# A new order of the attention stage: contexts in groups, scores later behind the rows of maxima, three more additions per head group, the low half of the maxima from a reduction

## The reference

```python
q = (x @ Wq).reshape(b, n, 4, 4, 32)       # 4 groups of 4 heads, head size 32
k = (x @ Wk).reshape(b, n, 4, 32)
v = (x @ Wv).reshape(b, n, 4, 32)
scores = einsum('bqgsd,bkgd->bgsqk', q, k) / sqrt(32)     # causal: keys behind the query are -inf
attn = softmax(scores, axis=-1)
ctx = einsum('bgsqk,bkgd->bqgsd', attn, v)
```

## Time and profile before

| | |
|---|---|
| median of 3 runs | 2770.99 us (2770.24 to 2773.05) |
| the profiled execution | 2771.73 us, its span 2770.0 us |
| PE busy | 2589.9 us, 93% |
| DVE, ACT, POOL busy | 1713.5, 1436.7, 982.6 us |
| mean granted TensorE clock | 0.96 of full speed |

### The profile page before, as it was taken

The page is one execution under the profiler, slowest core; times in us unless marked ns, Lnnn a source line. Parts: engine busy times, 40 slices in busy tenths (PEclk is TensorE's granted clock), DMA queues, the critical chain, the costliest instruction groups (busy, mean ns, idle before and its releaser), DMA issues. The chain is left out here.

```text
span 2770.0 us, 40600 instructions
## 1 busy us (share of the span) xinstructions
PE 2589.9 (93%) x14178; PEld 1808.6 (65%) x14178; DVE 1713.5 (62%) x3567; ACT 1436.7 (52%) x2768; POOL 982.6 (35%) x601
## 2 busy tenths in 40 slices
PE   6997999999999999999696999999999999699998
PEld 5784545454555545553475788888788888588886
DVE  3225777777777777783496544446554454467776
ACT  1221546555555556565487555556554554345453
POOL 6000455655565656566693000000000000245554
PEclk9996999999999999999897999999999999899999
DMA  6444012121111111110597323225432332675453
GB/s 216 163 163 115 22 34 60 44 60 41 49 47 43 49 49 47 43 33 9 172 347 253 112 85 115 100 91 177 135 111 80 114 103 88 217 254 162 124 164 103
DMA packets 204212, 304.34 MB, mean 110 GB/s; under 512 B 39376, under 2 KB 85488, under 8 KB 199792
## 3 DMA queue, kind: packets, MB, share of 16 engines
q1 hardware_dynamic: 200768, 294.72, 34.0%
q0 software_dynamic: 1600, 5.24, 0.5%
q10 hardware_dynamic: 1648, 1.88, 0.2%
HBM read 184.83 MB, written 116.42 MB: 109 GB/s over the span
## 5 line engine op out<-in xcount | busy, mean ns | idle before, releaser
L782 ACT ACTIVATE p_probs<-p_ps_s 128x512 f32<-128x512 f32 (+3 forms) x1280 | 598.3, 537 | 420.6 <-PE p_ps_s L715 413.4
L809 DVE TENSOR_REDUCE p_parts<-p_ps_m 128x1 f32<-128x512 f32 x768 | 477.4, 681 | 126.7 <-PE p_ps_m L703 126.0
L703 PE MATMUL p_ps_m<-p_k_m,p_q 96*128 96x512 f32 (+3 forms) x1280 | 480.2, 405 | 25.2 <-DMA p_q<-q_t 11.7
L715 PE MATMUL p_ps_s<-p_q,p_k_e 98*128 98x512 f32 (+3 forms) x1280 | 461.5, 386 | 29.1 <-DMA p_q<-p_rows 21.8
L672 POOL TENSOR_TENSOR p_added<-p_added,p_probs 128x2048 f32<-128x2048 f32 x88 | 403.2, 4582 | 32.5 <-ACT p_probs L782 23.9
L703 PEld LDWEIGHTS p_ps_m<-p_k_m,p_q 96*128 96x128 f32 x1280 | 247.8, 198 | 234.9 <-DVE p_parts L809 93.8
L715 PEld LDWEIGHTS p_ps_s<-p_q,p_k_e 98*128 98x128 f32 x1280 | 243.3, 195 | 161.9 <-ACT p_probs L782 70.3
L1671 POOL MEMSET p_power<- 128x1 f32 x1 | 0.1, 98 | 891.0 <-POOLq L1849 891.0
L733 PE MATMUL p_ps_c<-p_probs,p_v 128*32 128x512 f32 (+3 forms) x2560 | 306.8, 552 | 1.1 <-ACT p_probs L782 0.7
L813 DVE CUSTOM_DVE_ANT_0 p_masked<-p_ps_m,p_mask 128x384 f32<-128x384 f32 (+3 forms) x512 | 226.2, 487 | 122.5 <-PE p_ps_m L703 120.2
L73 PE MATMUL p_ps_l<-p_xT_hi,p_mu_hi 128*128 128x512 f32 x512 | 207.7, 406 | 16.4 <-DVE p_xT_lo L1500 11.7
(11 more groups left out here) (181 smaller groups left out, 4678.7 us busy)
## 6 DMA issues: line engine op xcount, KB each, us to landing
logits_t<-p_logit SPq DMA_DIRECT2D x32, 1024.0 KB, 5.0
p_lg<-logits_t SPq DMA_DIRECT2D x128, 256.0 KB, 3.7
p_q<-q_t SPq DMA_DIRECT2D x96, 256.0 KB, 4.7
p_w_raw<-L_ffn_W_dram SPq DMA_DIRECT2D x64, 256.0 KB, 5.4
p_so<-slot_out SPq DMA_DIRECT2D x32, 512.0 KB, 6.6
p_x<-L_attn_x_dram SPq DMA_DIRECT2D x8, 1024.0 KB, 6.3
q_t<-p_f_hi SPq DMA_DIRECT2D x32, 256.0 KB, 2.5
q_t<-p_f_lo SPq DMA_DIRECT2D x32, 256.0 KB, 2.6
```

The costliest lines, as they stand in the source:

```text
L703: pe.matmul(ps_m[:, u % M_BANKS, 0:w], q[0:QROWS, qb, h, bass.ts(t, P)], k_m[:, c * BLK:c * BLK + w], start=True, stop=True).then_inc(s_un ...
L715: pe.matmul(ps_s[:, u % ST_BANKS, q0:BLK], k_e[:, bass.ts(kt, P)], q[:, qb, h, q0:BLK], start=True, stop=True).then_inc(s_score, 1)
L782: act.activation(probs[s % RING][:, h, q0:BLK], ps_s[:, u % ST_BANKS, q0:BLK], ACT.Exp).then_inc(s_exp, 1)
L809: dve.tensor_reduce(to, bank, AX.X, ALU.max).then_inc(s_taken, 1)
```

## The change

- `ADDED`: one more step of each block with qb 1, 2, 3 is summed by POOL (additions per iteration 3 + 6 + 8 in place of 2 + 5 + 7), and its product with ones goes.
- `maximum_rows`: the subtraction of two SBUF tensors is replaced. The negated maximum and the rounded maximum are written as pairs, and one reduction adds each pair. There are three reductions of the parts in place of two, and the fourth one makes the low half.
- `Clock` and `plan`: other costs, new conditions. The rows of maxima are taken to be ready 950 + 5400 ns behind the last maximum of the block in place of 850 + 2300 ns. A group of packed items begins when both ACT and DVE have work for `fed` = 1300 ns, or the ring is full but one, or nothing else is ready; it goes on while its streaming time stays within `longest` = 1700 ns (or nothing else is ready). Cost of an order is all that changes here; no instruction is added or left out by it.

```diff
-ADDED = [[], [0, 1, 2], [0, 1, 2, 4, 5, 6], [0, 1, 3, 4, 6, 7, 9, 10]]
+ADDED = [[], [0, 1, 2, 3], [0, 1, 2, 3, 4, 5, 6], [0, 1, 2, 3, 4, 5, 6, 7, 9]]
...
-    HOP, LAND, ENTER, LEAVE = 90, 200, 86, 114
+    HOP, LAND, ENTER, LEAVE, AGAIN = 90, 200, 140, 114, 105
+    SHORT = {P: 110, 2 * P: 123, 3 * P: 177, 4 * P: 233}
...
     def packed_products(self, ready, columns, count):
-        self.pe = max(self.pe, ready) + count * 1.6 * columns + (0 if self.packed else self.ENTER + self.LEAVE)
+        first = 0 if self.packed else self.ENTER
+        self.run = 0.0 if first else self.run
...
+        self.run += count * 1.62 * columns
+        self.pe = max(self.pe, ready) + count * 1.62 * columns + first
         self.packed = True
...
         if u + 1 in M_END:
-            self.dve += 850
-            self.rows[n] = self.dve + 2300
+            self.dve += 950
+            self.rows[n] = self.dve + ROWS
...
+ROWS = 5400
+def context_time(s):
+    return (1 if is_added(s) else 2) * 1.62 * (BLK - first_query(s))
...
-def plan():
+def plan(fed=1300, lead=300, longest=1700, idle=50, press=1, near=20):
...
-        now = [x for x in ((k.act + 300, scores, 0), (k.dve, maximum, 1)) if x[1] <= k.pe + 40]
-        if packed <= k.pe and (not now or s - c >= RING - 2):
+        length = 830 if owed is not None else context_time(c) if c < s else 0
+        now = [x for x in ((k.act + lead, scores, 0), (k.dve, maximum, 1)) if x[1] <= k.pe + near]
+        if packed <= k.pe + 60 and (k.run + length <= longest or not now if k.packed else
+                                    min(k.act, k.dve) - k.pe >= fed or s - c >= RING - press or not now and min(scores, maximum) > k.pe + idle):
             what = 2
         elif now:
             what = min(now)[2]
         else:
-            what = min((scores, 0), (maximum, 1), (packed, 2))[1]
+            what = min((scores, 0), (maximum, 1), (packed if packed > k.pe + 60 or min(scores, maximum) > k.pe + idle else INF, 2))[1]
...
-                dve.tensor_reduce(neg[:, :], parts[n % 2][:, :, 0:qb + 1], AX.X, ALU.max, negate=True).then_inc(s_neg, 1)
-                dve.tensor_reduce(split[:, 0:16], parts[n % 2][:, :, 0:qb + 1], AX.X, ALU.max, negate=True).then_inc(s_neg, 1)
-                dve.wait_ge(s_neg, 3 * n + 2)
-                dve.tensor_tensor(split[:, 16:32], neg[:, :], split[:, 0:16], ALU.subtract).then_inc(s_neg, 1)
-                dve.wait_ge(s_neg, 3 * n + 3)
+                part = parts[n % 2][:, :, 0:qb + 1]
+                dve.tensor_reduce(pairs[:, :, 0], part, AX.X, ALU.max, negate=True).then_inc(s_neg, 1)
+                dve.tensor_reduce(pairs[:, :, 1].bitcast(F32R), part, AX.X, ALU.max).then_inc(s_neg, 1)
+                dve.tensor_reduce(split[:, 0:16], part, AX.X, ALU.max, negate=True).then_inc(s_neg, 1)
+                dve.wait_ge(s_neg, 4 * n + 3)
+                with nc.allow_low_precision(reason="the rounded low half of a sum of two"):
+                    dve.tensor_reduce(split[:, 16:32], pairs[:, :, :], AX.X, ALU.add).then_inc(s_neg, 1)
+                dve.wait_ge(s_neg, 4 * n + 4)
```

More of the change, by code:

```diff
@@ L368 @@
 class Clock:
-    HOP, LAND, ENTER, LEAVE = 90, 200, 86, 114
+    HOP, LAND, ENTER, LEAVE, AGAIN = 90, 200, 140, 114, 105
+    SHORT = {P: 110, 2 * P: 123, 3 * P: 177, 4 * P: 233}
     def __init__(self):
         self.pe = self.act = self.dve = self.pool = 0.0
-        self.packed = False
+        self.packed, self.again, self.run = False, False, 0.0
         self.maxed, self.scored, self.expd, self.chosen, self.summed = {}, {}, {}, {}, {}
@@ L378, in __init__ @@
         self.work, self.moves = [], []
+        self.groups, self.stall = 0, {"m": 0, "s": 0, "c": 0}
     def matmul(self, ready, columns):
-        self.pe = max(self.pe, ready) + max(64, 0.452 * columns + 3) + (self.LEAVE if self.packed else 0)
-        self.packed = False
+        if self.packed:
+            self.pe += self.LEAVE
+        extra = self.AGAIN if self.again else 0
+        self.again, self.packed = self.packed, False
+        self.wait = max(0, ready - self.pe)
+        self.pe = max(self.pe, ready) + self.SHORT[columns] + extra
         return self.pe + self.LAND
     def packed_products(self, ready, columns, count):
-        self.pe = max(self.pe, ready) + count * 1.6 * columns + (0 if self.packed else self.ENTER + self.LEAVE)
+        first = 0 if self.packed else self.ENTER
+        self.run = 0.0 if first else self.run
+        self.groups += first > 0
+        self.stall["c"] += max(0, ready - self.pe)
+        self.run += count * 1.62 * columns
+        self.pe = max(self.pe, ready) + count * 1.62 * columns + first
         self.packed = True
@@ L411, in maximum @@
         width = unit_width(u)
-        self.dve = max(self.dve, self.matmul(self.maximum_ready(u), width) + self.HOP) + 85 + 1.045 * width + (85 if c == BLOCKS[n][1] else 0)
+        scored = self.matmul(self.maximum_ready(u), width)
+        self.stall["m"] += self.wait
+        self.dve = max(self.dve, scored + self.HOP) + 1.042 * width + (79 if c == BLOCKS[n][1] else 65)
         self.maxed[u] = self.dve
@@ L428, in scores @@
         self.scored[u] = self.matmul(self.scores_ready(s, h), columns)
+        self.stall["s"] += self.wait
         begin = max(self.act, self.scored[u] + self.HOP)
@@ L473, in inverse @@
     def inverse(self, n):
-        self.flipped[n] = max(self.dve, self.pe + self.LAND + self.HOP) + 710
-        self.dve = self.flipped[n] + 1000
-        self.pool = max(self.pool, self.dve + self.HOP) + 1300
+        self.flipped[n] = max(self.dve, self.pe + self.LAND + self.HOP) + 740
+        self.dve = self.flipped[n] + 940
+        self.pool = max(self.pool, self.dve + self.HOP) + 1290
         self.work += [("inverse", n, None), ("normalise", n, None)]
@@ L541, in attention @@
         masked = [al.sbuf(f"p2_masked{r}", [P, BLK]) for r in range(4)]
-        neg = al.sbuf("p2_neg", [P, 16])
+        pairs = al.sbuf("p2_pairs", [P, 16, 2])
         split = al.sbuf("p2_split", [P, 32], F32R)
```

## The result

The changed kernel takes 2704.06 us (median of 4 runs, 2701.52 to 2706.36) against 2771.01 us (4 runs, 2770.24 to 2773.05): a ratio of 0.9757, interval 0.974 to 0.9774, 67 us faster. 2697 was predicted. Its profiled execution took 2706.36 us, with a span of 2704.2.

A forecast was written before the change was run, and what follows sets the result against it. PE was taken to bound attention. Additions 18, groups 27, stalls and clock 26, head 4, tail -1 made 74 us off 2771.7, so 2697.7, median 2697; own range 2674 to 2721, eight in ten 2673 to 2738.

The forecast's parts named there:

- PE sets the time: Attention's regular part, seven periods: PE busy 895.3 of 918.5 us, so the gain depends on PE time removed.
- More additions: Attention blocks: three ones products fewer per iteration save 18 us of PE over seven periods; sums don't wait for POOL.
- Groups: Packed matmuls in attention's seven periods: 88 fewer changes to and from unpacked at 0.31 us each, 27 us.
- DVE becomes the bound: Rival for attention's periods: each of 30 groups leaves DVE idle 1 us, period 127.5, time 2745; chance 0.10.
- Stall and clock: Seven periods: planning the rows of maxima later removes PE's waits for them and the clock loss behind; 26 of 36 us.
- The subtraction: Low half of the maxima on DVE: replacing it gains DVE 21 us, worth nothing directly, but shortens the rows' chain.
- Head and tail: Attention's start and end: 4 us gained in the first, 1 us lost in the last, which ends on POOL.
- small ends: Least gains taken for the five terms of the total: 18, 18, 15, 2 and -3, giving 2721.
- stall and clock stay if the reduction is held: Rival at the rows of maxima: reduction over pairs held, or scores too late for PE's contexts; 26 us lost, 2723; chance 0.12.

## Why the prediction was right, and where it wasn't

**PE sets the time: right in the main.** The freed PE time became time, and PE is shown busy for 826.2 of 826.4 us. Not all of that is its own work: halving the reductions took 1.9 us from each period, so short waits for DVE are in it.

**More additions, 18 us less 1 in the tail: right in mechanism.** The slack ahead of the sums was used up but not overrun: inside the periods PE waits for no addition. Undoing it costs 12.7 us, 2.3 us a period where 2.6 was counted with the product alone.

**Groups, 27 us: right in size when undone, less when done.** A regular iteration went from 43 groups to 32, where I had counted 30. At 0.34 us each these 11 groups are 3.7 us a period, for 3.9 forecast (12.6 groups at 0.31). The price is what two pairs of kernels show in which only the groups are undone. The step from the old order shows less, as the table below has it: the new order brings waits for banks of some 1.6 us a period that the old one didn't have (maxima pitches of 0.259 for 0.238 us). The page "TensorEngine Tiling (Array Packing)", section "Performance Considerations", of the Trainium skill, which says that copying PSUM out may be the next limit, was weighed as a rival (DVE becomes the bound, 0.10). The waits for banks go that way, but at 1.6 us a period they leave PE the bound. In the last iteration groups lose some 5 us. PE and ACT wait for each other there (from 1190 us on PE 3.4 us in 12 places, ACT 21.6 in 20), and which of them is the limit wasn't isolated.

**Stall and clock, 26 us: gone to the last bit, but the reason was wrong.** All 8 stalls and the 0.02 of the clock are gone in the regular part, 36 us by the prediction's rows and not 26. The planner's later rows, to which I gave this, are worth 8 us, all in the first iteration. The new order removes the stalls also with the rows believed early, also without groups, and also with the subtraction held. Which of its other costs and conditions does it wasn't taken apart.

**The subtraction, "worth nothing directly, since DVE isn't the bound": the step that failed.** It is worth 13 us in the old order and 58 in the new one. A share of busy time of 76% (79% in the changed kernel) says that DVE has time to spare on average. With three banks, a hold of 2 to 4.5 us is longer than what PE had in reserve in the place shown, PE's fixed order makes everything else wait behind one maximum, and the granted clock can fall behind the wait. The old order, with 28 us of holding, lost less than half of that; that it hid part beside stalls of its own is a guess.

**Head and tail.** In the prediction's own cut (the first scores of blocks 3 and 31, at 353.91 and 1210.11 us of the changed kernel's trace) the head gave 9.7 us for 4, the seven periods 62.3 for 71 (122.3 us each), and the tail lost 1.7 for 1. In the first 139.57 us PE's idle time fell from 17.3 to 7.5 us, which the prediction had not booked as a gain.

**The sum.** Where the time of the five iterations between the takes of blocks 7 and 27 went, in us. The clock's share is half of the time granted at 0.50, an upper estimate, since matmuls there took somewhat less than twice as long:

| step | five iterations | PE idle | clock | rest |
|---|---|---|---|---|
| before, to the changed kernel | -44.8 | -16.2 | -13.7 | -14.9 |
| subtraction back in the changed kernel | +38.1 | +21.4 | +13.7 | +3.1 |
| subtraction back, old additions (the plan alone) | +50.7 | +28.5 | +22.2 | 0.0 |
| pairs in the kernel before | -6.1 | -2.4 | -3.4 | -0.3 |
| groups undone in the changed kernel | +18.9 | -0.2 | 0.0 | +19.1 |
| additions undone in the changed kernel | +11.3 | -0.2 | 0.0 | +11.5 |

Idle time and clock were forecast at 26 us for seven periods, 18.6 for five; they gave 29.9. Additions and groups were forecast at 45, 32 for five; the rest gave 14.9. Undone singly they are worth 30 together. Of the missing 17 the waits for banks are 8 (1.6 a period) and the smaller number of groups 2 to 3; the others aren't accounted for. So the forecast of 74 came out near 67 in part by luck: too little was booked for the stalls, the clock and the head, and too much for what the new order takes off PE. The range also rests on small ends of 18 for the groups and 15 for the stalls, where the parts themselves had named 0 and 5.

The parts aren't additive. Undone one at a time from the changed kernel they cost 12.7 + 58 + 7.8 + 13.0 = 92 us for a total of 67; done step by step from the kernel before, pairs give 12.7 us, additions on top 25 (0.9954 to 0.9863), the plan on top of both 29. The additions are worth more in the old order because its stalls shrink with them (18.3 to 9.9 us of waits for the rows from 360 to 1190 us). Four of the kernels have the old additions and cross the other two parts:

| old additions | old plan | new plan |
|---|---|---|
| subtraction | 1 | 1.0028 |
| reductions over pairs | 0.9954 | 0.9803 |

The plan loses 8 us with the subtraction and gains 42 with the pairs. Of the rivals, "stall and clock stay if the reduction is held" was nearest to what binds the parts together, at 26 us where 58 were at stake; but the way was another, since it is the bank and not the rows that PE waits for. Why the same number of additions holds the subtraction longer in the new order (62.0 for 34.2 us) is open: it may meet an addition in progress more often or earlier in it, but no run moved the two apart.

## What to carry to other kernels

An engine that is 76 to 79% busy can cost the bound engine one for one, if one of its instructions may be held for longer than the buffers between the two last. Count what the clock loses behind such waits too. Look at the longest duration of each small instruction, not at the mean of the engine. Here an order fixed by a planner with better costs was worth its gain only once no instruction had a duration that the planner couldn't know: take out the variable one first. Grouping paid where PE was the bound and not in the last iteration, so read head, period and tail apart. Divide a count by where it changed, not by the whole: 79 groups over eight iterations were 11 in each regular one.

## What the runs showed of the hardware that I had not expected

- A 16-column subtraction of two SBUF tensors on DVE took up to 4.48 us beside GpSimd's additions, 2.0 us on average in the changed kernel's order; a reduction over pairs that makes the same values 0.186 us, never more than 0.188 in the changed kernel.
- A change from unpacked to packed matmuls and back costs TensorE 0.34 us, by the slope over 11 groups a period, twice (3.8 and 3.7 us).
- TensorE shown 100% busy at full clock still had 1.9 us in a period of 122.8 that a shorter reduction on DVE took away, hidden under overlapping records.
- With the subtraction back, 21.4 us more of idle time of PE in five iterations went with a granted clock of 0.50 for 27 us in seven places, which is worth up to 14 us more.
- The same list of work took 178.6 us in one kernel's head and 182.8 in another's, with a granted clock of 1.00 and 0.94 from 300 to 380 us.
- Stages with the same code took between 1432.1 and 1439.4 us behind attention in different kernels' profiled executions, more than the effect of several edits here. Differences below some 7 us are better read inside the stage that changed.
